# Vision tower block on one core: from the second group on, DMAs spread the C rows over the partitions, and the planner's clock follows more dependencies

## The reference, cut to what matters

```
h = embed(x)                                   # 768 -> 192
h = h + ssm_block(layernorm(h))                # per image, 36 tokens in order
h = h + experts(layernorm(h))                  # top 4 of 16, SwiGLU
...
xdbl = z @ W_xproj.T                           # 384 -> 96 + 16 + 16
dt_in, Bm, Cm = split(xdbl, [96, 112])
dt = softplus(dt_in @ W_dt.T + b_dt)
A_bar = exp(dt[..., None] * -exp(A_log))       # 384 channels x 16 states
Bx = (dt * z)[..., None] * Bm[:, :, None, :]
h_t = A_bar_t * h_{t-1} + Bx_t
y = einsum('blds,bls->bld', h, Cm) + D_skip * z
```

## Time and profile before

| | |
|---|---|
| runs (3) | median 626.79 us, 625.78 to 630.82 |
| profiled execution | 627.44 us, of it the span from the first to the last instruction 625.6 |
| mean granted TensorE clock | 0.945 of 2.4 GHz |
| PE busy | 557.0 us (89%), 3361 matmuls |
| PEld busy | 479.1 us (77%) |
| DVE busy | 475.5 us (76%) |
| ACT busy | 295.2 us (47%) |
| POOL busy | 388.3 us (62%) |
| DMA | 88.34 MB, queue of SP busy 43.4% of 16 engines |

### The profile page before, as it was taken

One profiled execution on the slowest core, in us unless ns is written; L12 is line 12 of the kernel. 1 busy time (PEld: TensorE's weight loads), 2 busy tenths in 40 slices (PEclk: granted clock), 3 DMA queues, 4 the chain that ended last, 5 costly groups with the idle time before them and its releaser, 6 DMA issues.

```text
span 625.6 us, 10398 instructions
## 1 busy us (share of the span) xinstructions
PE 557.0 (89%) x3361; PEld 479.1 (77%) x3361; DVE 475.5 (76%) x897; ACT 295.2 (47%) x699; POOL 388.3 (62%) x447
## 2 busy tenths in 40 slices
PE   3959589977899999989999997999998889978896
PEld 3748478866698988879887885988886768857785
DVE  1166868889789789979879996999989556565664
ACT  1167846483544475544446474445442324323442
POOL 3257777767456458857555984767677355564674
PEclk9779959989899999999999997999999889997999
DMA  9993533432053343413343341554342266553781
GB/s 238 308 299 97 164 119 90 189 135 92 1 155 100 106 155 95 162 33 112 111 171 112 105 141 46 135 157 143 121 177 88 50 207 213 178 174 104 238 274 52
DMA packets 41827, 88.34 MB, mean 141 GB/s; under 512 B 9581, under 2 KB 34477, under 8 KB 35501
## 3 DMA queue, kind: packets, MB, share of 16 engines
q1 hardware_dynamic: 41772, 87.68, 43.4%
HBM read 77.24 MB, written 10.40 MB: 140 GB/s over the span
## 4 chain that ended last, share of the span: by engine, by line
PE 61%; DVE 15%; issue 6%; DMA 6%; ACT 5%; POOL 4%; SPq 2%; POOLq 0%; DVEq 0%; ACTq 0%
PE post L770 12%; PE y_sum L770 10%; PE sums L770 10%; PE gate_up L770 10%; PE pre L770 8%; PE linear_up L770 8%; DVE state L1255 4%; DMA w<-w_store 3%; PE fills L770 3%; DVE fills L1246 2%; DVE dts L1222 2%; SPq L709 1%; POOL read L1456 1%; DMA hid<-patches 1%; DVE scratch L1354 1%
## 5 line engine op out<-in xcount | busy, mean ns | idle before, releaser
L1456 POOL TENSOR_TENSOR read<-state,c_all 128x504 f32<-128x504 f32 (+1 forms) x120 | 147.0, 1228 | 83.2 <-DVE state L1255 54.8
L1255 DVE TENSOR_TENSOR_SCAN state<-a_bar,fills 128x504 f32<-128x504 f32 (+1 forms) x120 | 133.0, 1109 | 12.1 <-ACT a_bar L1035 4.1
L1485 POOL TENSOR_TENSOR scratch<-scratch 128x252 f32<-128x252 f32 (+1 forms) x120 | 81.6, 680 | 87.4 <-DVE scratch L1369 82.4
L770 PE MATMUL y_sum<-read,ident 128*128 128x252 f32 (+1 forms) x480 | 122.5, 382 | 4.1 <-POOL read L1456 3.7
L1035 ACT ACTIVATE scratch<-scratch 128x252 f32<-128x252 f32 (+1 forms) x120 | 47.3, 394 | 147.0 <-DVE scratch L1354 146.8
L770 PE MATMUL sums<-hid,w 128*128 128x252 f32 (+1 forms) x480 | 103.8, 377 | 4.8 <-POOL hid L1494 4.8
L770 PE MATMUL gate_up<-t_high,w 128*128 128x252 f32 (+1 forms) x360 | 89.3, 318 | 14.5 <-DVE route L1332 7.2
L770 PEld LDWEIGHTS y_sum<-read,ident 128*128 128x128 f32 x480 | 86.3, 201 | 19.8 <-issue 7.1
L1035 ACT ACTIVATE a_bar<-dts,decay 128x245 f32<-128x245 f32 (+1 forms) x240 | 100.2, 470 | 2.2 <-DVE dts L1230 2.2
L1494 POOL TENSOR_TENSOR hid<-scratch,route_rows 128x252 f32<-128x252 f32 (+1 forms) x120 | 84.9, 708 | 14.4 <-DMA route_rows<-mix_rows 7.6
L770 PE MATMUL linear_up<-t_high,w 128*128 128x252 f32 (+1 forms) x360 | 85.8, 308 | 2.3 <-ACT mix_w L1035 1.7
(11 more groups left out here) (166 smaller groups left out, 851.9 us busy)
## 6 DMA issues: line engine op xcount, KB each, us to landing
w<-w_store SPq DMA_DIRECT2D x40, 1152.0 KB, 5.7
route_rows<-mix_rows SPq DMA_DIRECT2D x192, 63.0 KB, 3.0
w_store<-w SPq DMA_DIRECT2D x8, 1152.0 KB, 5.0
scratch<-expert_w SPq DMA_DIRECT2D x16, 384.0 KB, 5.6
w<-expert_w SPq DMA_DIRECT2D x1, 2304.0 KB
route_rows<-mix_rows SPq DMA_DIRECT2D x48, 36.0 KB, 2.8
w_embed<-embed_w SPq DMA_DIRECT2D x3, 256.0 KB, 3.9
x_patch<-patches SPq DMA_DIRECT2D x1, 756.0 KB, 5.0
```

The source lines that it names most:

```text
L770: return nc.tensor.matmul(out, lhsT, rhs, start=start, stop=stop, skip_group_check=shared, is_transpose=turned)
L1255: dve.tensor_tensor_scan(pair(state, i, c), pair(a_bar, i, c), pair(fills, i, c), 0.0, ALU.mult, ALU.add).then_inc(scanned.sem, 1)
L1456: pool.tensor_tensor(by_state(pair(read, i, c)), by_state(pair(state, i, c)), c_all[:, n:n + 2, 0:tok(c)], ALU.mult).then_inc(read_out.sem, 1)
L1485: pool.tensor_tensor(glu[:, 0:tok(c)], product[un % 2][:, 0:tok(c)], g_one[un % 2][:, 0:tok(c)], ALU.mult)\
```

## The change

From group 1 on nothing is spread on PE. After `bc_copy`, SP stores the 16 C rows of `bc` to DRAM (`c_store`), and loads them back eight times, two rows repeated over 128 partitions each time, straight into `c_all` (`c_load`). Load p waits until the store has landed and until read 16 + p of the group before is done. POOL's read of these states waits for the load. Group 0 goes on as before. The two waits that stood for "the bank is free" (`embed`, `outproj`) go by the softplus copies of `delta_abs` instead.

In the planner the loads are a stream of their own, placed over the last seven places before the group's scan. The clock gets a lane "D" for DMAs, lets each step start only when all that `needed` names has ended, scales a cost by the group's tokens with a fixed part for each engine (before, a quarter for all), weighs waits with 0.87, and has changed costs and spans.

```diff
-def before_scan():
+def before_scan(c):
...
-    turns += [[("xproj", 0), ("dt_in", 0)], [("bc_copy", 0), ("bc_high", 0)],
+    turns += [[("xproj", 0), ("dt_in", 0)], [("bc_copy", 0)] + ([("c_store", 0)] if c else []) + [("bc_high", 0)],
...
+    if c:
+        return [[("c_load", p)] for p in range(C_PAIRS)]
     return [[("c_spread", p), ("c_copy", p)] for p in range(C_PAIRS)]
...
-        return [(0, "square", 0) if c == 1 else (c - 1 if c > 2 else 0, "c_copy", C_PAIRS - 1)]
+        return [(0, "square", 0) if c == 1 else (0, "c_copy", C_PAIRS - 1) if c == 2 else (c - 1, "delta_abs", 1)]
...
+    if step == "drive_b" and i == 0:
+        return [(c, "drive", 0)]
     if step == "read":
-        return [(c, "c_copy", i)] if i < STEPS_PER_BLOCK else []
+        return [(c, "c_load" if c else "c_copy", i)] if i < STEPS_PER_BLOCK else []
...
+    if step == "c_load":
+        return [(c, "c_store", 0), (c - 1, "read", SCAN_STEPS - STEPS_PER_BLOCK + i)]
...
+            for f in needed(c, step, i):
+                ready = max(ready, end.get(f, ended.get(f, 0.0)))
...
-                at[engine] = start + us * (0.25 + 0.75 * size)
+                at[engine] = start + us * (FIXED[engine] + (1.0 - FIXED[engine]) * size)
...
-            p = SCAN_STEPS * (c - 1)
-            places = spread_over(len(b), p, p + BEFORE_SPAN) + spread_over(len(s), p + 17.0, p + 24.0)
+            p = SCAN_STEPS * (c - 1) + BEFORE_FROM
+            places = spread_over(len(b), p, p + BEFORE_SPANS[c])
+        if c:
+            loads += list(zip(s, spread_over(len(s), SCAN_STEPS * c - 7.0, SCAN_STEPS * c)))
...
-    "poly": (("V", .7),), "log1p": (("V", .72),), "drive": (("G", 2.2),), "c_spread": (("P", .25),),
+    "poly": (("V", 0.9),), "log1p": (("V", 0.85),), "drive": (("G", 2.2),), "c_spread": (("P", .25),),
...
+    "split_w1": (("S", 1.), ("G", 2.)), "c_store": (("D", .1),), "c_load": (("D", 1.2),),
...
-LATENCY = {"P": 0.22, "V": 0.12, "S": 0.1, "G": 0.14}
-WAIT_WEIGHT = 0.5
-BEFORE_SPAN = 15.5
-AFTER_SPAN, LAST_AFTER_SPAN = 20.9, 22.0
-EXPERT_SPAN, LAST_EXPERT_SPAN = 25.1, 21.7
+FIXED = {"P": 0.08, "V": 0.22, "S": 0.5, "G": 0.22, "D": 0.2}
+LATENCY = {"P": 0.22, "V": 0.12, "S": 0.1, "G": 0.14, "D": 2.5}
+WAIT_WEIGHT = 0.87
+BEFORE_FROM = -1.1
+BEFORE_SPANS = (23.32, 9.14, 24.58, 17.43, 16.28)
+AFTER_SPANS = (20.9, 20.9, 20.2, 20.99, 23.78)
+EXPERT_SPANS = (25.1, 25.1, 22.68, 23.26, 34.27)
...
+            def c_store(c, _):
+                sp.wait_ge(bc_copied.sem, bc_copied.at(c, 1))
+                sp.dma_start(c_rows[c % 2][0, :, 0:tok(c)], bc[STATES:2 * STATES, 0:tok(c)]).then_inc(c_kept.sem, 16)
+
+            def c_load(c, p):
+                if p == 0:
+                    sp.wait_ge(c_kept.sem, c_kept.at(c, 0))
+                sp.wait_ge(read_out.sem, read_out.at(c - 1, SCAN_STEPS - STEPS_PER_BLOCK + p + 1))
+                sp.dma_start(c_all[:, 2 * p:2 * p + 2, 0:tok(c)],
+                             c_rows[c % 2][:, 2 * p:2 * p + 2, 0:tok(c)].to_broadcast([P, 2, tok(c)]))\
+                    .then_inc(c_in[p].sem, 16)
...
+                    elif c == 2:
+                        pe.wait_ge(c_ready.sem, c_ready.at(0, C_PAIRS))
                     else:
-                        pe.wait_ge(c_ready.sem, c_ready.at(c - 1 if c > 2 else 0, C_PAIRS))
+                        pe.wait_ge(v_max.sem, v_max.at(c - 1, NJ))
...
-                        pe.wait_ge(c_ready.sem, c_ready.at(1, C_PAIRS))
+                        pe.wait_ge(v_max.sem, v_max.at(1, NJ))
...
             def bc_copy(c, _):
                 dve.wait_ge(pe_xproj.sem, pe_xproj.at(c, 1))
+                if c > 1:
+                    dve.wait_ge(c_kept.sem, c_kept.at(c - 1, 0))
...
                 if i < STEPS_PER_BLOCK:
-                    pool.wait_ge(c_ready.sem, c_ready.at(c, i + 1))
+                    if c:
+                        pool.wait_ge(c_in[i].sem, c_in[i].at(c, 0))
+                    else:
+                        pool.wait_ge(c_ready.sem, c_ready.at(0, i + 1))
```

More of the change, by code:

```diff
@@ L113, in before_scan, with c_turns @@
     return turns + [[("log1p", 0), ("drive", 0)]]
-def c_turns():
+def c_turns(c):
+    if c:
+        return [[("c_load", p)] for p in range(C_PAIRS)]
     return [[("c_spread", p), ("c_copy", p)] for p in range(C_PAIRS)]
@@ L207, in needed @@
     if step == "c_spread":
-        return [(c, "log1p", 0)] + ([(c - 1, "read", SCAN_STEPS - STEPS_PER_BLOCK + i)] if c else [])
+        return [(c, "log1p", 0)]
+    if step == "c_load":
+        return [(c, "c_store", 0), (c - 1, "read", SCAN_STEPS - STEPS_PER_BLOCK + i)]
     if step == "outproj":
-        return [(c, "y", NJ - 1), (1, "c_copy", C_PAIRS - 1) if not c else (c - 1, "t_low", 0)]
+        return [(c, "y", NJ - 1), (1, "delta_abs", 1) if not c else (c - 1, "t_low", 0)]
     if step == "scale3":
@@ L240, in schedule @@
     out, given, ended = [], set(), {}
-    free = {"P": 4.0, "V": 4.0, "S": 10.0, "G": 4.0}
+    free = {"P": 4.0, "V": 4.0, "S": 10.0, "G": 4.0, "D": 4.0}
     streams, reading = [], [0.0]
@@ L276, in lay @@
         return waits, max(end.values())
-    prep = []
+    prep, loads = [], []
     for c in range(NC):
-        b, s = of_cut(c, before_scan()), of_cut(c, c_turns())
+        b, s = of_cut(c, before_scan(c)), of_cut(c, c_turns(c))
         if c == 0:
@@ L283, in schedule @@
         elif c == 1:
-            places = spread_over(len(b), -16.0, 20.0) + spread_over(len(s), 17.0, 24.0)
+            places = spread_over(len(b), -16.0, 20.0)
         else:
-            p = SCAN_STEPS * (c - 1)
-            places = spread_over(len(b), p, p + BEFORE_SPAN) + spread_over(len(s), p + 17.0, p + 24.0)
+            p = SCAN_STEPS * (c - 1) + BEFORE_FROM
+            places = spread_over(len(b), p, p + BEFORE_SPANS[c])
+        if c:
+            loads += list(zip(s, spread_over(len(s), SCAN_STEPS * c - 7.0, SCAN_STEPS * c)))
         if c == 1:
-            stream(b + s, places)
+            stream(b, places)
         else:
-            prep += list(zip(b + s, places))
-    streams.append(prep)
+            prep += list(zip(b + s if not c else b, places))
+    streams += [prep, loads]
     scans = []
@@ L342 @@
     "embed": (("P", .87),), "embedded": (("S", .9),), "mean": (("P", .85),), "center": (("V", .6),),
-    "square": (("S", .56),), "variance": (("P", .9),), "roots": (("V", .18),), "power": (("G", 1.),),
+    "square": (("S", 0.61),), "variance": (("P", .9),), "roots": (("V", .18),), "power": (("G", 1.),),
     "spread": (("P", .45),), "scale": (("V", 1.5),), "inproj": (("P", 1.7),),
-    "gate": (("S", .32),), "z": (("V", .38),), "xproj": (("P", 1.27),), "dt_in": (("S", .45),),
+    "gate": (("S", 0.37),), "z": (("V", .38),), "xproj": (("P", 1.27),), "dt_in": (("S", .45),),
     "bc_copy": (("V", .36),), "bc_high": (("S", .36),), "bc_low": (("V", .4),), "delta": (("P", .65),),
     "delta_abs": (("S", 1.2),), "delta_exp": (("S", .75),), "factor": (("S", .9),),
-    "poly": (("V", .7),), "log1p": (("V", .72),), "drive": (("G", 2.2),), "c_spread": (("P", .25),),
-    "c_copy": (("S", .52),), "decay": (("S", .82),), "fill": (("P", .25),), "drive_b": (("V", .6),),
-    "advance": (("V", 1.13),), "read": (("G", 1.2),), "collect": (("P", .85),), "y": (("V", .43),),
-    "outproj": (("P", 1.27),), "y1_add": (("V", .6),), "square2": (("S", .62),), "variance2": (("P", .9),),
+    "poly": (("V", 0.9),), "log1p": (("V", 0.85),), "drive": (("G", 2.2),), "c_spread": (("P", .25),),
+    "c_copy": (("S", 0.57),), "decay": (("S", 0.8),), "fill": (("P", .25),), "drive_b": (("V", 0.62),),
+    "advance": (("V", 1.15),), "read": (("G", 1.26),), "collect": (("P", .85),), "y": (("V", .43),),
+    "outproj": (("P", 1.27),), "y1_add": (("V", .6),), "square2": (("S", 0.62),), "variance2": (("P", .9),),
     "roots2": (("V", .18),), "power2": (("G", 1.),), "spread2": (("P", .23),),
-    "scale2": (("V", .78),), "ffn_up": (("P", 1.7),), "ffn_tanh": (("S", .36),), "ffn_product": (("V", .78),),
+    "scale2": (("V", .78),), "ffn_up": (("P", 1.7),), "ffn_tanh": (("S", 0.37),), "ffn_product": (("V", .78),),
     "down": (("P", 1.7),), "h1": (("V", .55), ("G", 1.25)), "mean3": (("P", .85),), "center3": (("V", .58),),
@@ L500, in vit_tower @@
         mix_rows = [nc.dram_tensor(f"mix_rows{k}", [EXPERTS, TM], F32).ap() for k in range(2)]
+        c_rows = [nc.dram_tensor(f"c_rows{k}", [1, STATES, TM], F32).ap() for k in range(2)]
         w1_store = nc.dram_tensor("w1_store", [PAIRS, P, 3, PAIR_COLS], F32).ap()
@@ L550, in vit_tower @@
         c_ready = signal("c_ready", C_PAIRS)
+        c_kept = signal("c_kept", 1, 16)
+        c_in = [signal(f"c_in{p}", 1, 16) for p in range(C_PAIRS)]
         pe_b = signal("pe_b", SCAN_STEPS)
@@ L861, in c_spread @@
             def c_spread(c, p):
-                if not c and p == 0:
+                if p == 0:
                     pe.wait_ge(picks_rounded.sem, 1)
-                if p == 0:
```

15 lines of the change are left out of this document (6 added, 9 removed).

## The result

The changed kernel takes 642.18 us (median of 4 runs, 641.64 to 643.44) against 626.98 us for the kernel before in the same session: ratio 1.0255 (95% interval 1.0211 to 1.0299). It is slower by 15 us where 16 us less were forecast, and the time lies above the end of the range, 630.

What follows compares the result with a forecast made beforehand. PE was taken to set the pace in scans 2 to 4, DVE in scan 1, a web of waits in scan 0. 627.4 - 10.9 - 5 = 611.5, so 611 us for the median; range 596 to 630 for eight of ten.

Steps and rivals of the forecast that it cites:

- Part 2: C's store and loads by DMA: 4 us per load, hidden by the scan's steps; SP's waits cost 0.
- SP stands in the way: Rival, scans 2 to 4: C loads come late or hold up weight loads, costing 12 us, time 623; chance 0.05.
- Part 1: No spreading for groups 1 to 4: scan 0 5.0, scan 1 1.5, scans 2 and 3 2.2 each; 10.9 us less.
- the five intervals: Scan 0's last steps, 83.28 to 97.19: 2.78 us each, at most 6.6 us less at the early 1.47 us pace.
- the first rival: Hidden anyway: removed matmul pairs in scans 2 and 3 only lengthen PE's waits; 4 us go, time 623; chance 0.17.
- the sum of 615: Scans 2 and 3 judged by PE's weight loads: PE has room, both 2.2 us terms are 0, time 615 us.
- Part 3: The planner's new order leaves less idle time: a sixth of 29.4 us idle PE from scan 2 on, 5 us less.
- group 2 is ready too late: Rival between scans 1 and 2: group 2's preparation chain sticks out by 14.3 us, time 635; chance 0.12.

Runs made afterwards that it cites:

- e9: The kernel before plus nine waits on SP (DVE's group 1 copy, last eight reads of scan 0), no DMA added: 640.85 us, ratio 1.0246.
- e5: The changed kernel with raw expert-weight loads 3 to 14 moved in SP's program right behind the split that frees their tile: 619.56 us, ratio 0.9893.
- e13: The kernel before, order kept, C spreading of groups 1 to 4 replaced by SP's store and loads, raw loads first: 629.93 us, ratio 1.0036.
- e3: The changed kernel (C by DMA) with the planner's clock, costs, weights and spans of before: 649.04 us, ratio 1.0381.
- e4: e3 with raw expert-weight loads 7 to 14 moved ahead in SP's program: 640.03 us, ratio 1.0224.
- e6: e3 with raw expert-weight loads 3 to 14 moved ahead in SP's program, as in e5: 630.89 us, ratio 1.0052.
- e2: The changed kernel's new planner, but C spread by PE and ACT for all groups as before: 640.43 us, ratio 1.0228.
- e12: e5 with the late spans of the planner before (617.31 us), and then also its preparation spans: 614.25 us, ratio 0.9819.

## Why the prediction was wrong

**The step that failed: Part 2, the queue.** The text says "behind it in SP's program stand the route loads, the weight loads and the result stores" and costs the wait at 0. That list holds for scans 2 to 4. In scans 0 and 1 the raw loads of the split stand there, and group 1's C path is put exactly there; neither the text nor the account of SP's DMAs ahead of it has them. The rival "SP stands in the way" had the mechanism, with the wrong victim (weight loads in scans 2 to 4; PE waits 3.2 us for them after, 4.6 before), a price of 12 us and a chance of 0.05. Measured: 15.4 us for the waits alone on the kernel before (e9), 22.6 us given back by the move (e5). Little in the profile of before marks these loads: ACT waited 1.7 us in all for one of them, and the one followed above was issued 16.9 us ahead of its split. A list of waits doesn't show slack.

**Part 2, the rest: right.** A C load landed in 3.6 us (median; 3.0 to 7.6), the estimate was 4 with ends 3.0 and 5.7. The slowest lay above the upper end, but no read of POOL waits for a load. The loads' own traffic is no cause (e9).

**Part 1 (-10.9): wrong in size, and without a term for the clock.** With the order kept (e13) the time moved not by -10.9 us but by +0.4%, some 2 us. Term by term, in the profiled execution: scan 0 -2.1 where -5.0 was taken, scan 1 +1.0 (-1.5), scan 2 +1.2 and scan 3 +0.7 (-2.2 each). In scan 0 the mechanism was right: from step 16 to step 23 the time fell from 18.3 to 13.4 us, as forecast. But from step 23 to the next scan it rose from 3.2 to 6.2, where DVE waits 4.7 us for PE's fills, so the gain was partly taken back at the join. The text had counted this join among the five intervals that would go back to the early pace: its last row, at 97.19 with 504 columns, is scan 1's first step.

For scans 2 and 3 the sum held the granted clock fixed. By length times clock, as in e3, e4 and e6 (an estimate, with clocks of two digits), e13's scan 2 comes to 103.3 us against 105.4 before, and scan 3 to 111.9 against 112.4: some 2 us and half a microsecond less at the same clock, where 2.2 each was taken. So it isn't shown that the pairs were hidden, as the first rival says, though PE's idle time did grow (2.5 to 3.8 us in scan 2, 4.4 to 5.2 in scan 3). The Trainium skill (Perfetto Trace Analysis, section Identifying the Most-Contended Engine) warns of the matmuls' busy share, on which these terms rest, and judges by the weight loads among others, which left 12 and 17% here. The bare lengths of e13 agree with it, and with the sum of 615; the three runs in which scan 2 follows PE's clock speak for a stage that PE paces. This stays open.

The whole kernel says the same of the sum. Two runs of e13 had clocks of 0.940 and 0.943 and took 623.99 and 623.49 us. The runs of the kernel before at 0.939 to 0.944 took 623.84 to 627.39, with a median of 625.5. At the same clock e13 is some 2 us faster, not 11.

**Part 3 (-5): right in sign beside the DMA path, and not a term of its own.** With the stall away, the DMA path is at 1.0036 with the old order (e13) and at 0.9893 with the new one (e5): 9 us less. Part of that is the clock: in scan 2 it was 0.96 in e13 and 1.00 in the new order. And not all of scan 2's 100.6 us is a gain. In the changed kernel, whose scans 2 to 4 are as long as e5's to 0.1 us, its records hold 645 matmuls where before there were 680, and only 16 of them are C's; scan 4, which is 5.6 us longer in e5 than before, holds 571 instead of 564. So other work left scan 2, and some of it went to scan 4. The new planner with the old path is 2.3% slower (e2). Neither half pays alone; a sum of separate terms could not show that.

**Rival "group 2 is ready too late": nearly nothing.** From step 23 of scan 1 to the first step of scan 2 pass 7.7 us instead of 4.9; 2.8 us, not 14.3, and the old spans give 3.1 back (e12).

**Open.** What sets the clock in a stage wasn't tried. In e6 it fell to about half for some 11 us of scan 2, with PE busy all of that time, and in e4 at the same place of the same order it did not. Why the removed work is worth so little in e13 at the same clock is known only in part (the join behind scan 0).

## What to carry to other kernels

Before a wait is put on an engine that issues DMAs, list what stands behind it in that engine's program in each stage of the kernel, also what runs ahead and shows no wait: its slack is the time from its issue to its use, less its landing (here 16.9 - 5.6, some 11 us), and a new wait that is longer stalls the engine that uses it. Issue loads in the order in which they become possible; here that alone turned 2.5% slower into 1.1% faster. A planner that sets such an order would need a lane for the issuing engine with its waits, not only for the transfers; this was not tried. And before two profiles are compared stage by stage, put the granted clock of the stage beside its length.
